# One attention stage of a four-block network: probabilities transposed on TensorE, or logits formed a second time with the keys on the partitions

## The chip, the cores and the metric

The kernel runs on one NeuronCore of a Trainium2 chip. The metric is the device time of one launch in microseconds, taken as the median of several runs. TensorE (PE) does the matrix products, VectorE (DVE), ScalarE (ACT) and GpSimd (POOL) the element-wise work, and SyncE (SP) issues the transfers.
## The reference, cut to what matters

The network is a chain of four blocks over `x` (4 batches, 512 tokens, 512 features). The changed stage is the attention of the third block. Its queries come from the 512 tokens of `x`, its keys and values from those tokens and 64 context tokens together, 576 keys in all, with 16 heads of 32 features:

```python
residual = latents                                  # x: 4 x 512 x 512
h = jnp.concatenate([x, latents], axis=1)           # context and tokens: 576 rows
q = (latents @ q_w + q_b).reshape(b, k_len, NH, DH)            # NH = 16, DH = 32
kv = (h @ kv_w + kv_b).reshape(b, p + k_len, NH, DH, 2)
attn = jnp.einsum('bkhd,bnhd->bhkn', q, kmat) / DH
attn = jnp.where(full_mask[:, None, None, :], attn, -jnp.inf)  # hides some context keys
attn = jax.nn.softmax(attn.astype(jnp.float32), axis=-1)
attn_out = jnp.einsum('bhkn,bnhd->bkhd', attn, v).reshape(b, k_len, H)
attn_out = attn_out @ out_w + out_b + residual
```

## The kernel before

The network is a list of stages, each ended by a barrier of all engines. The function `l2_attention_stage` is one of them; its tiles show in the trace without the 2 of their names (`l_slot`, `l_probs`). Its work is one loop of four passes, one a batch. In a batch the tokens are transposed into `source` (features on the partitions), and then four groups of four heads follow, `m` = 0 to 3. For each group `project` forms the queries and keys of 128 features, ACT copies them out of PSUM, and DVE (`split`) makes a rounded float32r part and the rest of each. SP copies these parts into `q_stack` and `k_stack`, 24 transfers a group (28 with the mask row, in the first group of a batch), so that for each head 96 partitions hold high, low and high parts one under another and one float32r product of 97 rows gives a logit of nearly float32 accuracy.

For each head `i` and each tile `t` of 128 queries, `logits` (L1021) makes a tile of 128 queries by 576 keys in two halves of 288 in one of two places of `slot`. DVE takes the maximum of each row (L1162), and ACT the exponential with that maximum as its bias (L1110), which also adds up the row. The values need the probabilities with the keys on the partitions, so TensorE turns them: `turn` (L1033) makes four transposes of 128 by 128 for each of five chunks of keys, and ACT (chunks 0, 2 and 4, L1133) and DVE (chunks 1 and 3, L1205) copy them out. `mix` (L1045) then multiplies a chunk with `padded_v`, a 128-wide copy of the values in which only the 32 columns of the head are not zero, so that four heads add up in one PSUM bank `gathered`. The sums of the rows are inverted while they are small (128 by 16, L1179), spread and turned once a group (`turn_inverse`, L1054), and multiplied in (L1190). At the end of a batch `project_out` (L1063) multiplies with `wo`; DVE adds the residual rows (L1218), and SP stores them.

The order on TensorE is written out by hand. Inside a head it alternates the logits of the next head, the transposes of this one and the values of the one before. The list of TensorE is that of the loops at the end of its block:

```python
for c in range(CHUNKS):
    if c < TPB and i + 1 < H:
        logits(b, i + 1, c)
    if i < H:
        turn(b, i, c)
    if i >= 1:
        mix(b, i - 1, c)
```

## Time and profile before

| what | us |
|---|---|
| median of 3 runs (3251.75 to 3257.56) | 3254.83 |
| the profiled execution, its own time | 3249.24 |
| its span in the profile | 3247.4 |
| TensorE busy in the span | 2958.6 (91%) |
| VectorE busy | 1538.0 (47%) |
| ScalarE busy | 938.5 (29%) |

The profile is of one execution. A busy time counts every instruction from its start to its modelled end, and matrix instructions overlap, so the distance between the starts of two instructions that follow each other without a wait tells what the first one costs the engine; the printed duration is longer. A printed group merges neighbours of one kind and gives their number after an x. The changed stage lies between 1370 and 2176 us of the span, a quarter of it.

### The profile page before, as it was taken

The numbers are of one execution on the slowest core, as the hardware profiler recorded it, in microseconds if no ns is written. First come the engines' busy times: TensorE is split into PE (matmuls) and PEld (weight loads), VectorE is DVE, ScalarE is ACT, GpSimd is POOL, SyncE is SP. The second block draws the span as 40 slices with busy tenths as digits, with TensorE's granted clock in tenths as the row PEclk, the third lists the DMA queues.
The fourth block names the chain that finished last, engine by engine and source line by source line (L and its number), as shares of the span: only waits on it lengthen the run. The fifth ranks groups of instructions, "written<-read, shape, count | busy, mean of one in ns | idle before, by whom it ended". The sixth has DMA issues, their size and how long they took to land. (4 is left out here: it accounts for less than half of the span.)

```text
span 3247.4 us, 34409 instructions
## 1 busy us (share of the span) xinstructions
PE 2958.6 (91%) x12408; PEld 2142.5 (66%) x12408; DVE 1538.0 (47%) x2345; ACT 938.5 (29%) x1914; POOL 177.0 (5%) x122
## 2 busy tenths in 40 slices
PE   6999979999979999899999999977999879779999
PEld 4776747777668887456465564646888635458887
DVE  3555454444674442236254463546444454564443
ACT  4223323333131111145254452533111112231111
POOL 2000001000040000000000000004000030021000
PEclk9999979999889999899999999998999999889999
DMA  3111011110010002122111221221000101110001
GB/s 128 40 52 52 0 56 52 53 52 1 1 56 26 26 1 88 38 55 57 48 43 49 59 52 55 47 74 55 26 27 1 56 24 39 59 68 27 26 1 52
DMA packets 63704, 139.72 MB, mean 43 GB/s; under 512 B 33298, under 2 KB 33427, under 8 KB 51795
## 3 DMA queue, kind: packets, MB, share of 16 engines
q1 hardware_dynamic: 46930, 137.52, 12.7%
q10 hardware_dynamic: 16640, 0.39, 0.2%
q8 instruction: 87, 1.43, 0.2%
q14 instruction: 47, 0.38, 0.0%
HBM read 82.89 MB, written 8.45 MB: 28 GB/s over the span
## 5 line engine op out<-in xcount | busy, mean ns | idle before, releaser
L1045 PE MATMUL l_gathered<-l_probs_T,l_padded_v 128*128 128x512 f32 x640 | 325.0, 594 | 0.0
L1162 DVE TENSOR_REDUCE l_top<-l_slot 128x1 f32<-128x576 f32 x256 | 192.5, 757 | 278.3 <-PE l_slot L1021 277.8
L1110 ACT ACTIVATE l_probs<-l_slot,l_top 128x576 f32<-128x576 f32 x256 | 190.0, 742 | 166.7 <-DVE l_top L1162 165.9
L1021 PE MATMUL l_slot<-l_k_stack,l_q_stack 128*128 128x288 f32 x512 | 192.7, 457 | 18.7 <-ACT l_probs L1110 16.2
L1033 PE MATMUL l_turned<-ident,l_probs 128*128 128x128 f32 x1280 | 193.4, 273 | 4.3 <-ACT l_probs_T L1133 4.3
L1033 PEld LDWEIGHTS l_turned<-ident,l_probs 128*128 128x128 f32 x1280 | 154.7, 140 | 50.2 <-ACT l_probs_T L1133 25.7
L1021 PEld LDWEIGHTS l_slot<-l_k_stack,l_q_stack 128*128 128x128 f32 x512 | 92.7, 190 | 128.7 <-issue 84.1
L470 PE MATMUL l0a_wide<-l0a_key_map,l0a_norm 128*128 128x260 f32 x512 | 118.7, 385 | 9.3 <-DVE l0a_soft L623 7.2
L470 PE MATMUL l0b_wide<-l0b_key_map,l0b_norm 128*128 128x260 f32 x512 | 118.7, 385 | 9.3 <-DVE l0b_soft L623 7.2
L1678 ACT ACTIVATE l2m_hidden<-l2m_up,columns 128x512 f32<-128x512 f32 x64 | 44.2, 692 | 270.1 <-PE l2m_up L131 263.9
L1678 ACT ACTIVATE l0m_hidden<-l0m_up,columns 128x512 f32<-128x512 f32 x64 | 44.0, 694 | 268.4 <-PE l0m_up L131 261.3
L1678 ACT ACTIVATE l3m_hidden<-l3m_up,columns 128x512 f32<-128x512 f32 x64 | 44.0, 694 | 268.4 <-PE l3m_up L131 261.3
L1133 ACT COPY l_probs_T<-l_turned 128x512 f32<-128x512 f32 x192 | 111.2, 579 | 25.3 <-PE l_turned L1033 19.1
L470 PEld LDWEIGHTS l0b_wide<-l0b_key_map,l0b_norm 128*128 128x128 f32 x512 | 95.6, 190 | 27.6 <-DVE l0b_soft L623 9.8
L470 PEld LDWEIGHTS l0a_wide<-l0a_key_map,l0a_norm 128*128 128x128 f32 x512 | 95.6, 190 | 27.6 <-DVE l0a_soft L623 9.8
L129 PE MATMUL l2m_up<-l2m_norm_hi,l2m_w1h 128*128 128x512 f32 x256 | 101.4, 396 | 8.4 <-DVE l2m_norm_lo L1742 8.4
L129 PE MATMUL l3m_up<-l3m_norm_hi,l3m_w1h 128*128 128x512 f32 x256 | 100.7, 394 | 7.1 <-DVE l3m_norm_lo L1742 7.1
L129 PE MATMUL l0m_up<-l0m_norm_hi,l0m_w1h 128*128 128x512 f32 x256 | 100.7, 393 | 7.1 <-DVE l0m_norm_lo L1742 7.1
L1045 PEld LDWEIGHTS l_gathered<-l_probs_T,l_padded_v 128*128 128x128 f32 x640 | 97.9, 191 | 10.5 <-issue 10.5
L130 PE MATMUL l2m_up<-l2m_norm_lo,l2m_w1h 128*128 128x512 f32 x256 | 100.8, 394 | 0.0
L131 PE MATMUL l2m_up<-l2m_norm_hi,l2m_w1l 128*128 128x512 f32 x256 | 100.6, 393 | 0.0
L130 PE MATMUL l0m_up<-l0m_norm_lo,l0m_w1h 128*128 128x512 f32 x256 | 100.3, 392 | 0.0
(369 smaller groups left out, 6314.4 us busy)
## 6 DMA issues: line engine op xcount, KB each, us to landing
l_k_stack<-l_k_parts SPq DMA_DIRECT2D x192, 72.0 KB, 2.0
l_q_stack<-l_q_parts SPq DMA_DIRECT2D x192, 64.0 KB, 2.0
l0m_raw<-in_weights SPq DMA_DIRECT2D x8, 1024.0 KB, 4.9
l_rows<-x SPq DMA_DIRECT2D x8, 1024.0 KB, 4.7
l2m_raw<-in_weights SPq DMA_DIRECT2D x8, 1024.0 KB, 7.0
l3m_raw<-in_weights SPq DMA_DIRECT2D x8, 1024.0 KB, 4.8
x<-in_x SPq DMA_DIRECT2D x4, 1024.0 KB, 9.4
l0a_wk<-in_weights SPq DMA_DIRECT2D x4, 1024.0 KB, 5.1
```

The lines of the kernel that those rows point to most:

```text
L129: pe.matmul(out, lh, rh, start=start, stop=False)
L130: pe.matmul(out, lh, rl, start=False, stop=False)
L131: return pe.matmul(out, ll, rh, start=False, stop=stop)
L470: last = pe.matmul(wide[:, j, 0:W], norm[:, k, at:at + P], key_map[:, k, b, :, :].rearrange("p h c -> p (h c)"), start=k == 0, stop=k == K ...
L1021: last = pe.matmul(out[:, half, 0:HALF], q_stack[:, j, t * P:(t + 1) * P], k_stack[:, j, half * HALF:(half + 1) * HALF], start=True, stop= ...
L1033: last = pe.transpose(turned[:, bank, t * P:(t + 1) * P], probs[:, i % 2, t, first:first + P], n.ident[:, :])
L1045: last = pe.matmul(gathered[:, m % 2, :], padded_v[:, c, j, :], probs_T[:, i % 2, c, :], start=(j == 0 and c == 0), stop=(j == 3 and c == ...
L1110: act.activation(probs[:, i % 2, t, :].rearrange("p (a k) -> p a k", a=2), slot[:, u % 2, :, 0:HALF], ACT.Exp, bias=top[:, i % 2, t:t + 1] ...
L1133: act.copy(probs_T[:, i % 2, c, :], turned[:, 0, :]).then_inc(s["turned0_out"], 1)
L1162: dve.tensor_reduce(top[:, i % 2, t:t + 1], slot[:, u % 2, :, 0:HALF], AX.XY, ALU.max, negate=True).then_inc(s["top_ready"], 1)
L1678: act.activation(hidden[:, i % 2, :], up[:, m, :], activation, bias=n.col(bias, f * KT + m))\
```

## The change

The loop over batches is written out, with groups numbered 0 to 15 through all batches (`g`). The logits are still formed with the queries on the partitions, in tiles of 128 by 576 (`logits`), but only to take the maxima; their place in `slot` is free once DVE has read it. The negated maxima of the four heads of a group are split into two float32r parts, turned by TensorE (`turn_tops`) and copied by ACT into rows 97 and 98 of `q_stack` (`take_tops`), where rows of ones in `k_stack` stand against them. A second product, `logits_across`, has the keys of a chunk as its stationary side and 512 queries moving, and so gives logit minus maximum with the keys on the partitions. ACT takes the exponential of a chunk of one head (128 keys by 512 queries) and writes it to `weighed`. The transposes of the probabilities, both kinds of copy out of `turned`, and `padded_v` are gone.

`mix` multiplies a chunk with the values of one head, 32 columns wide, into the 32 partitions of `gathered` that belong to the head, and then with 32 columns of ones into `totals`: eight products of 32 columns a chunk and group, where there were four of 128 columns. The reciprocal is taken of `totals`, 128 by 512, on DVE (`normalise`). The stacks have two halves, `g % 2`; SP fills the half of group `g + 2` once the last `logits_across` of group `g` is done, and TensorE waits for all transfers of a half at once. The mask row is loaded in the first two groups of a batch. The input is turned straight from `n.x`, GpSimd adds the bias to the residual rows, and DVE adds the value bias.

The diff, cut to its core:

```diff
...
-        stack_loaded = [n.sem(f"{tag}_stack{j}_loaded") for j in range(4)]
+        weighed = n.sbuf(f"{tag}_weighed", [P, RING, 4, S], F32, mem)
+        top = n.sbuf(f"{tag}_top", [P, TPB, 4], F32, mem)
+        top_parts = n.sbuf(f"{tag}_top_parts", [P, TPB, 4, 32], F32, mem)
+        inverse = n.sbuf(f"{tag}_inverse", [P, S], F32, mem)
+        slot = n.psum(f"{tag}_slot", [P, 4, 512], mem)
+        across = n.psum(f"{tag}_across", [P, 2, S], mem)
+        gathered = n.psum(f"{tag}_gathered", [P, S], mem)
...
+            def load_stack(g):
+                a, b, m = g % 2, g // GROUPS, g % GROUPS
+                sp.wait_ge(s["parts_ready"], g + 1)
+                if g >= 2:
+                    sp.wait_ge(s["across_done"], USES * (g - 1))
+                for j in range(4):
+                    mine = slice(32 * j, 32 * j + 32)
+                    for c in range(3):
+                        third = slice(32 * c, 32 * c + 32)
+                        sp.dma_start(q_stack[third, a, j, :].bitcast(F32), q_parts[mine, c // 2, :].bitcast(F32)).then_inc(stack_loaded[a], 16)
+                        sp.dma_start(k_stack[third, a, j, :].bitcast(F32), k_parts[mine, c % 2, :].bitcast(F32)).then_inc(stack_loaded[a], 16)
+                    if m < 2:
+                        sp.dma_start(k_stack[ROW:ROW + 1, a, j, S:KEYS].bitcast(F32),
+                                     mask[:, b * C:(b + 1) * C].bitcast(F32)).then_inc(stack_loaded[a], 16)
 
             sp.dma_start(keep[:, :], n.dram["keep_l2"]).then_inc(s["consts_loaded"], 16)
...
+            def turn_tops(g):
+                use = USES * g
+                pe.wait_ge(s["top_split"], g + 1)
+                if use:
+                    pe.wait_ge(s["across_read"], use - 1)
+                for t in range(TPB):
+                    last = pe.transpose(across[:, use % 2, t * P:(t + 1) * P],
+                                        top_parts[:, t, :, :].rearrange("p h c -> p (h c)"), n.ident[:, :])
+                last.then_inc(s["across_done"], 1)
+
+            def logits_across(g, c, j):
+                use = USES * g + 1 + 4 * c + j
+                pe.wait_ge(s["across_read"], use if c == 0 and j == 0 else use - 1)
+                pe.matmul(across[0:height(c), use % 2, :], k_stack[0:LAST, g % 2, j, keys_of(c)], q_stack[0:LAST, g % 2, j, :],
+                          start=True, stop=True).then_inc(s["across_done"], 1)
+
+            def mix(g, c):
+                m, tall = g % GROUPS, height(c)
                 if c == 0:
-                    pe.wait_ge(s["slot_read"], b * SLOTS + slot_of_logits(i, TPB - 1) + 3)
-                at = b * T1 + 2 * i + max(0, (i - 1) // 4) + c // 2 if bank else b * T0 + 3 * i + c // 2
-                pe.wait_ge(s[f"turned{bank}_out"], at + 1)
-                first = min(c * P, KEYS - P)
-                for t in range(TPB):
-                    last = pe.transpose(turned[:, bank, t * P:(t + 1) * P], probs[:, i % 2, t, first:first + P],
-                                        n.ident[:, :])
-                last.then_inc(s[f"turned{bank}_done"], 1)
-
-            def mix(b, i, c):
-                m, j = i // 4, i % 4
-                if c == 0:
-                    pe.wait_ge(s["padded_ready"], b * H + i + 1)
-                    pe.wait_ge(s["turned0_out"], b * T0 + 3 * i + 4)
-                    pe.wait_ge(s["turned1_out"], b * T1 + 2 * i + max(0, (i - 1) // 4) + 3)
-                    if j == 0:
-                        pe.wait_ge(s["gathered_read"], b * GATHERED + m + 1)
-                last = pe.matmul(gathered[:, m % 2, :], padded_v[:, c, j, :], probs_T[:, i % 2, c, :],
-                                 start=(j == 0 and c == 0), stop=(j == 3 and c == CHUNKS - 1))
-                if c == CHUNKS - 1:
-                    last.then_inc(s["gathered_done"], 1)
-
...
+            for g in range(ALL):
+                m, b = g % GROUPS, g // GROUPS
+                for c in range(CHUNKS):
+                    for j in range(4):
+                        logits_across(g, c, j)
+                        if c < TPB and g + 1 < ALL:
+                            logits(g + 1, TPB * c + j)
+                    if c:
+                        mix(g, c - 1)
+                if m == 1 and b + 1 < B:
+                    turn_input(b + 1)
+                if g + 3 < ALL:
+                    pe.wait_ge(s["top_ready"], TILES_OF * (g + 2))
+                    project_q(g + 3)
+                mix(g, CHUNKS - 1)
+                if g + 3 < ALL:
+                    project_k(g + 3)
+                if g + 1 < ALL:
+                    turn_tops(g + 1)
+                if m == GROUPS - 1:
...
+            def take_tops(g):
+                use = USES * g
+                act.wait_ge(s["across_done"], use + 1)
+                for j in range(4):
+                    last = act.copy(q_stack[ROW:LAST, g % 2, j, :], across[32 * j:32 * j + LAST - ROW, use % 2, :])
+                last.then_inc(s["across_read"], 1)
+
+            def exps(g, c):
+                if CHUNKS * g + c >= RING:
+                    act.wait_ge(s["mix_done"], CHUNKS * g + c - RING + 1)
+                for j in range(4):
+                    use = USES * g + 1 + 4 * c + j
+                    act.wait_ge(s["across_done"], use + 1)
+                    act.activation(weighed[0:height(c), (CHUNKS * g + c) % RING, j, :], across[0:height(c), use % 2, :], ACT.Exp)\
+                        .then_inc(s["across_read"], 1)
+
...
+            def split(g):
+                dve.wait_ge(s["k_out"], g + 1)
+                if g:
+                    dve.wait_ge(stack_loaded[(g - 1) % 2], loaded(g - 1))
                 dve.tensor_copy(q_parts[:, 0, :], projected[:, 0, 0:S])
-                dve.tensor_copy(k_parts[:, 0, :], projected[:, 1, :]).then_inc(s["parts_chain"], 1)
-                dve.wait_ge(s["parts_chain"], b * GROUPS + m + 1)
+                dve.tensor_copy(k_parts[:, 0, :], projected[:, 1, :]).then_inc(s["parts_high"], 1)
+                dve.wait_ge(s["parts_high"], g + 1)
                 dve.tensor_tensor(q_parts[:, 1, :], projected[:, 0, 0:S], q_parts[:, 0, :].bitcast(F32), ALU.subtract)
-                dve.tensor_tensor(k_parts[:, 1, :], projected[:, 1, :], k_parts[:, 0, :].bitcast(F32),
...
+            def split_tops(g):
+                dve.wait_ge(s["top_ready"], TILES_OF * (g + 1))
+                if g:
+                    dve.wait_ge(s["across_done"], USES * (g - 1) + 1)
+                dve.tensor_copy(top_parts[:, :, :, 1].bitcast(F32R), top[:, :, :]).then_inc(s["top_high"], 1)
+                dve.wait_ge(s["top_high"], g + 1)
+                dve.tensor_tensor(top_parts[:, :, :, 2], top[:, :, :], top_parts[:, :, :, 1], ALU.subtract).then_inc(s["top_split"], 1)
+
+            def normalise(g):
+                m, b = g % GROUPS, g // GROUPS
+                dve.wait_ge(s["mix_done"], CHUNKS * (g + 1))
+                dve.reciprocal(inverse[:, :], totals[:, :]).then_inc(s["inverse_ready"], 1)
+                dve.wait_ge(s["inverse_ready"], g + 1)
+                if b and m == 0:
+                    dve.wait_ge(s["out_done"], TPB * b)
+                dve.tensor_tensor(mixed[:, m, :], gathered[:, :], inverse[:, :], ALU.mult).then_inc(s["mixed_ready"], 1)
...
+            for g in range(ALL):
+                m, b = g % GROUPS, g // GROUPS
+                if g + 1 < ALL:
+                    for i in range(TILES_OF):
+                        maximum(g + 1, i)
+                    split_tops(g + 1)
+                normalise(g)
+                if g + 3 < ALL:
+                    split(g + 3)
+                if m == GROUPS - 1:
...
```

The order of instructions on TensorE. First the kernel before, inside one head: logits of the next head, transposes of this one, the values of the one before, and again.

```order
L1021 MATMUL l_slot<-l_k_stack,l_q_stack 128x288 x2
L1030 REGISTER_ALU
L1033 MATMUL l_turned<-ident,l_probs 128x128 x4
L1045 MATMUL l_gathered<-l_probs_T,l_padded_v 128x512
L976 REGISTER_ALU
L1021 MATMUL l_slot<-l_k_stack,l_q_stack 128x288 x2
```

The changed kernel, the end of one chunk and the beginning of the next one; a chunk has four such pairs of `l_across` and `l_slot`.

```order
L1032 MATMUL l_across<-l_q_stack,l_k_stack 128x512
L1015 MATMUL l_slot<-l_k_stack,l_q_stack 128x288 x2
L1032 MATMUL l_across<-l_q_stack,l_k_stack 128x512
L1015 MATMUL l_slot<-l_k_stack,l_q_stack 128x288 x2
L1044 MATMUL l_gathered<-l_weighed,l_values 32x512 x4
L1047 MATMUL l_totals<-l_weighed,l_ones 32x512 x4
L1032 MATMUL l_across<-l_q_stack,l_k_stack 128x512
```

The four transposes and the 128-wide product of each chunk and head have gone; a 512-wide product of the second logits has come in, and the values of four heads stand together as eight 32-wide products. At the end of a group TensorE now has these rows, from the last chunk (64 keys) on:

```order
L1032 MATMUL l_across<-l_q_stack,l_k_stack 64x512 x4
L1044 MATMUL l_gathered<-l_weighed,l_values 32x512 x4
L1047 MATMUL l_totals<-l_weighed,l_ones 32x512 x4
L967 MATMUL l_slot<-l_source,l_wq 128x512 x4
L1044 MATMUL l_gathered<-l_weighed,l_values 32x512 x4
L1047 MATMUL l_totals<-l_weighed,l_ones 32x512 x4
L975 MATMUL l_slot<-l_source,l_wk 128x288 x8
L1025 MATMUL l_across<-ident,l_top_parts 128x128 x4
L1032 MATMUL l_across<-l_q_stack,l_k_stack 128x512
L1015 MATMUL l_slot<-l_k_stack,l_q_stack 128x288 x2
```

The projections of a later group stand between the last values of a group and the turned maxima of the next; the row after the maxima, the first `l_across` of the next group, reads what ACT copies from them. On DVE the kernel before has this list where a group ends (`l_total` and `l_inverse` are 128 by 16, and the parts of a later group are split between the maxima):

```order
L1179 RECIPROCAL l_inverse<-l_total 128x16
L1180 ISA
L1181 COPY l_wide_inverse<-l_inverse 128x512
L1168 ISA
L1172 TENSOR_TENSOR l_padded_v<-l_values,l_bv_row 128x4x32
L1174 TENSOR_TENSOR l_padded_v<-l_values,l_bv_row 64x32
L1160 REGISTER_ALU
L1162 TENSOR_REDUCE l_top<-l_slot 128x1
```

And the changed kernel, one whole group:

```order
L1167 TENSOR_REDUCE l_top<-l_slot 128x1 x16
L1174 CAST l_top_parts<-l_top 128x16
L1176 TENSOR_TENSOR l_top_parts<-l_top,l_top_parts 128x16
L1181 RECIPROCAL l_inverse<-l_totals 128x512
L1185 TENSOR_TENSOR l_mixed<-l_gathered,l_inverse 128x512
L1151 CAST l_q_parts<-l_projected 128x512
L1152 CAST l_k_parts<-l_projected 128x576
L1154 TENSOR_TENSOR l_q_parts<-l_projected,l_q_parts 128x512
L1155 TENSOR_TENSOR l_k_parts<-l_projected,l_k_parts 128x576
```

The reciprocal has grown from 16 to 512 elements a partition, and it stands with the split of a later group ahead of the maxima of the next group but one.

## Rows read from the trace of the kernel before

**Rows 1.** Windows: busy us of each engine, TensorE's granted clock; the stage.

```profile
core 0: us, PE busy (x) PEld busy (x) DVE busy (x) ACT busy (x) POOL busy (x), PEclk, DMA share, GB/s
1370.00:2180.00 810.00, 761.78 (x3232) 468.05 (x3232) 384.19 (x661) 352.08 (x765) 7.65 (x4) 0.99 0.19 51
```

**Rows 2.** Timeline (start, us, instructions): the stage's first instruction and its last on DVE.

```profile
1369.86 1.80 POOL L963 MEMSET l_q_stack<- 32x2048 f32 x1 [399.88 <-POOLq L110]
...
2175.02 0.69 DVE L1218 TENSOR_TENSOR l_rows<-l_gathered,l_rows 128x512 f32<-128x512 f32 x1 [2.74 <-PE l_gathered L1063]
```

**Rows 3.** Costliest groups: busy us, mean ns of one, idle before and its releaser.

```profile
L1045 PE MATMUL l_gathered<-l_probs_T,l_padded_v 128*128 128x512 f32 x640 | 325.0, 594 | 0.0
L1162 DVE TENSOR_REDUCE l_top<-l_slot 128x1 f32<-128x576 f32 x256 | 192.5, 757 | 278.3 <-PE l_slot L1021 277.8
L1110 ACT ACTIVATE l_probs<-l_slot,l_top 128x576 f32<-128x576 f32 x256 | 190.0, 742 | 166.7 <-DVE l_top L1162 165.9
...
L1033 PE MATMUL l_turned<-ident,l_probs 128*128 128x128 f32 x1280 | 193.4, 273 | 4.3 <-ACT l_probs_T L1133 4.3
```

**Rows 4.** Timeline of TensorE in the stage's first batch, steady part and projections.

```profile
1442.60 0.82 PE L1021 MATMUL l_slot<-l_k_stack,l_q_stack 128*128 128x288 f32 x2
...
1444.15 0.83 PE L1021 MATMUL l_slot<-l_k_stack,l_q_stack 128*128 128x288 f32 x2
1444.82 0.60 PE L1033 MATMUL l_turned<-ident,l_probs 128*128 128x128 f32 x4
...
1446.12 0.60 PE L1033 MATMUL l_turned<-ident,l_probs 128*128 128x128 f32 x4
1446.55 1.02 PE L1045 MATMUL l_gathered<-l_probs_T,l_padded_v 128*128 128x512 f32 x2
1447.41 3.60 PE L1004 MATMUL l_slot<-l_source,l_wq 128*128 128x512 f32 x8
1450.85 4.04 PE L1009 MATMUL l_slot<-l_source,l_wk 128*128 128x288 f32 x16
1454.51 0.65 PE L1021 MATMUL l_slot<-l_k_stack,l_q_stack 128*128 128x288 f32 x2
```

**Rows 5.** Timeline of TensorE in the next stage: float32r products, 512 columns moving.

```profile
2211.54 0.39 PE L131 MATMUL l2m_up<-l2m_norm_hi,l2m_w1l 128*128 128x512 f32 x1
2211.77 0.39 PE L129 MATMUL l2m_up<-l2m_norm_hi,l2m_w1h 128*128 128x512 f32 x1
```

**Rows 6.** Timeline of TensorE in the first block: stationary data of 4 columns, then 128.

```profile
63.44 3.60 PE L452 MATMUL l0a_wide<-l0a_wo,l0a_learnt_v 128*4 128x512 f32 x8
66.97 2.00 PE L460 MATMUL l0a_wide<-l0a_keys,l0a_wqT 128*128 128x257 f32 x8
```

**Rows 7.** Groups by line: reciprocals on DVE, a copy on ACT.

```profile
L1179 DVE RECIPROCAL l_inverse<-l_total 128x16 f32<-128x16 f32 x16 | 4.0, 253 | 0.5
L822 DVE RECIPROCAL l_inverse<-l_total 128x4 f32<-128x4 f32 x4 | 0.7, 178 | 0.1
L1133 ACT COPY l_probs_T<-l_turned 128x512 f32<-128x512 f32 x192 | 111.2, 579 | 25.3 <-PE l_turned L1033 19.1
```

**Rows 8.** Timeline of DVE: start of a split, the instruction behind it, two maxima.

```profile
2098.24 0.43 DVE L1152 CAST l_q_parts<-l_projected 128x512 fp32r<-128x512 f32 x1
...
2100.35 0.68 DVE L1187 COPY l_inverse_T<-l_turned 128x512 f32<-128x512 f32 x1
...
2102.28 1.42 DVE L1162 TENSOR_REDUCE l_top<-l_slot 128x1 f32<-128x576 f32 x2
```

**Rows 9.** SP's queue: first and last of a group's 24 transfers; KB, us to landing.

```profile
1425.55 0.52 SPq L940 DMA_DIRECT2D l_q_stack<-l_q_parts  x1
...
1441.03 0.59 SPq L942 DMA_DIRECT2D l_k_stack<-l_k_parts  x1
l_k_stack<-l_k_parts SPq DMA_DIRECT2D x192, 72.0 KB, 2.0
```

**Rows 10.** Windows, columns as in rows 1: behind the first four logits tiles.

```profile
1409.00:1414.50 5.50, 5.34 (x10) 2.54 (x11) 0.56 (x3) 1.01 (x5) 0.00 (x0) 0.72 0.56 203
```

More of the change, by code:

```diff
@@ L904, in l2_attention_stage, with loaded, keys_of, height @@
+        def loaded(g):
+            return 16 * sum(24 + (4 if h % GROUPS < 2 else 0) for h in range(g % 2, g + 1, 2))
+        def keys_of(c):
+            return slice(c * P, min((c + 1) * P, KEYS))
+        def height(c):
+            return P if c < CHUNKS - 1 else C
         block = mem.enter_context(nc.Block())
@@ L1007, in project, with project_q, project_k @@
+            def project_q(g):
+                pe.wait_ge(s["source_ready"], 2 * (g // GROUPS + 1))
+                m = g % GROUPS
+                for k in range(KT):
+                    last = pe.matmul(slot[:, 0, :], wq[:, k, m * P:(m + 1) * P], source[:, k, 0:S], start=k == 0, stop=k == KT - 1)
+                last.then_inc(s["q_done"], 1)
+            def project_k(g):
+                pe.wait_ge(s["ctx_ready"], g // GROUPS + 1)
+                m = g % GROUPS
                 for half in range(2):
@@ new lines, in add_out @@
+            def add_out(b):
+                dve.wait_ge(s["rows_ready"], TPB * (b + 1))
+                for t in range(TPB):
+                    dve.wait_ge(s["out_done"], TPB * b + t + 1)
+                    dve.tensor_tensor(rows[:, t, :], slot[:, OUT_BANK[t], :], rows[:, t, :], ALU.add).then_inc(s["out_added"], 1)
+            split(0)
+            take_values(0)
+            split(1)
+            for i in range(TILES_OF):
+                maximum(0, i)
+            split_tops(0)
+            split(2)
```

416 lines of the change are left out of this document (157 added, 259 removed).

## The prediction

> **What bounds the kernel now.** I read the windows of the changed stage first, then its edges, the costliest groups, and the timeline of TensorE in its steady part. In the stage TensorE is busy 762 of 810 us at a granted clock of 0.99, VectorE 384 and ScalarE 352 [rows 1]: the stage is TensorE's. It runs from 1369.9 to 2175.7 us, 806 us [rows 2]. DVE's maxima wait 278 us for TensorE, and ACT's exponentials 166 us for DVE, while the costliest products wait for nothing [rows 3].
>
> In the steady part each step is read from the distance of two starts [rows 4]. Four transposes and one 128-wide float32 product of 512 columns (two instructions) follow each other at 1446.12, 1446.55 and 1447.41: 0.43 to 0.44 and 0.86 us. With a pair of logits products the round is 1.55 where without it is 1.30 (1444.82 to 1446.12): 0.26 for the pair. A query projection is 3.44, a key projection 3.66. So TensorE's own time in the stage is: 320 products of values at 0.86 = 275; 320 times four transposes at 0.44 = 141; 256 logits tiles at 0.26 = 67; 16 query and 16 key projections 55 + 59; value and output projections, 20 and 16 times eight instructions of 0.43, 69 + 55; input and inverse transposes 14. That is 735, and 806 - 735 leaves 71 us of waits and edges.
>
> **What goes and what comes on TensorE.** Transposes and 128-wide products of values go: -416 us. The other 319 us stay; the turned maxima replace the turned inverses one for one.
>
> The second logits are 320 float32r products with 512 columns moving. In the next stage two such products start 0.23 us apart [rows 5]: +74. Bounds: half of a float32 instruction's 0.43, so 0.21, and 0.30 if the change between products costs something; 67 to 96.
>
> The values are now 640 float32 products of 32 columns, 1280 instructions. This is the term that decides, and no row shows products that write different 32-column strips. The sum of TensorE is 319 + 74 + 291 = 684, 51 below before. Although the transposes are gone, the values cost 291 instead of 275, because the sums of the rows are now products too.
>
> The Trainium skill, "TensorE: Matmul & The Clock Gate", Part 3, says that column strips run concurrently with starts some 4 ns apart and gives 2.38x for three 32-wide products, but also that matrix instructions start and end strictly in program order. By the first sentence alone the stage would come out as in the four-at-once rival; by the second it comes out as forecast. No row here shows either.
>
> **What TensorE now waits for.** Durations come from rows; hand-overs (0.3 us from issue to a result, 0.1 for a semaphore) are estimates, since no row has this pattern. ACT's exponential of 512 columns lies between the copy of 512 (579 ns) [rows 7] and the exponential of 576 (742) [rows 3]: 0.69, repeated every 0.60. Maxima repeat every 0.66 (1.42 for two, 0.76 for one) [rows 3, 8].
>
> (a) The turned maxima. The first product across of a group reads what ACT copies from them: the key projection's copy (about 0.65) must be done, then four copies of 512 columns at 0.49 each. TensorE has 0.43 us of other work. It idles 2.75 us in 13 groups; in the other three the value and output projections cover it: 36.
> (b) Inside a chunk TensorE issues a pair of steps in 0.49, but both `across` and `slot` have two places. After two free steps the third waits 0.4 for the first exponential, the fourth 0.3 for the second maximum: 0.69 in 48 chunks = 33. The chunk of 64 keys has no logits beside it and goes at ACT's pace, 1.3 in 16 groups = 21; the last group has none at all, 4. Together 58. During the values (3.64) ACT and DVE catch up, so neither becomes the bound: DVE's list is 16 x 0.66 + 0.5 + 3.35 + 0.7 + 2.1 = 17 a group of some 42.
> (c) The start of a group on DVE and SP. A reciprocal of 16 elements takes 253 ns and of 4 178 [rows 7]: 6.25 ns an element, so 3.35 us for 512 (bounds 0.7, the price of a multiplication of that size, and 4). It, the multiplication and the split (2.11) [rows 8] stand ahead of the maxima of the next logits. The reciprocal is hidden by the key projection (3.66), the turned maxima and wait (a). The split is not: it waits for the same transfers as the logits. SP issues 24 in 1441.03 - 1425.55 + 0.6 = 16.1 us, landing 2.0 after issue [rows 9], so 17.5 to 18 us (28 of them: some 20) behind the last product across. TensorE comes to the logits after 3.64 + 3.44 + 3.64 + 3.66 + 0.43 + 2.75 + 0.23 = 17.8. So the logits start about in time or 2 us late, and the maxima 2 us behind that: 3 us in each of 12 groups, 35. Bounds 0 and 80: at 0.8 us a transfer instead of 0.64 each group would start 4 us later.
> (d) Ends. Input copies 4 x 1.6; the first 16 logits tiles stand alone at DVE's pace and cost 9 more than their issue; last reciprocal, multiplication and addition 6, others 2: 23.
>
> Waits are 36 + 58 + 35 + 23 = 152. The stage is 684 + 152 = 836 against 806: +30. ACT loses copies and row sums, which frees nothing, since TensorE does not wait for their absence. GpSimd's additions (16) and context copies lie beside TensorE's list. The profiled execution of 3249 becomes 3279; it lies 5.6 us below the median, so I add the difference to the median: 3254.8 + 30 = 3285.
>
> **Rivals.**
> *Four strips at once (faster).* Each half product of a head runs beside those of the other three, as though each strip had its own list. Place: the eight products at the end of a chunk. They cost 1.72 + 0.2, so TensorE's sum is 684 - 80 x 1.72 = 546. But the road to the logits of the next group is now 3.4 us shorter than the transfers, so (c) grows by some 30 to 65, and the waits to 182. The stage is 728, -78: 3177. It decides from a chunk below 3.3 us: with 80 chunks the 30 us are made up at 0.37 us a chunk. For it speaks that the stage gives each head its own 32 partitions of both banks; against it that the two halves of a float32 product stand next to each other in TensorE's list. The page named above, read for concurrency alone, says this rival.
> *Nothing overlaps.* The eight products cost 6.88 + 0.2, +275; (c) falls by 20, since the transfers are now covered: 836 + 255 = 1091 or, with more of (b) left open, up to 1100: 3254.8 + 290 = 3545. For it: the rows know only full serial products [rows 4, 6]. Against it: 32-row strips of one bank have no shared output.
> *The clock.* As forecast, but TensorE, idle more often, gets the lower clock. Behind the four sparse logits tiles at the start of the first batch the granted clock of the next 5.5 us was 0.72 [rows 10], where full speed would have saved some 1.5 of them. If each group pays 1.5 to 2 us so: +25 to 30, 3312. The whole stage had 0.99 though [rows 1], and the gaps of (a) and (c) are 3 us.
> *Less waiting than counted.* (a), (b) and (c) rest on hand-overs. If they were half, the stage would equal the one before: 3255 +- 6.
>
> The Trainium skill, "TensorEngine Tiling (Array Packing)", Key Properties, says that a change of tiling mode drains TensorE. Here the trace agrees in kind and has 0.1 us for it [rows 6], which is in the sum; with the 0.3 of the bound the sum would be 16 us more.
>
> **Chances and range.** Two at once, with its clock variant: 0.48 (own range 3265 to 3312). Four at once: 0.28. Nothing overlaps: 0.20. Less waiting: 0.04. What this kernel's measurement can tell from no change is 0.2%, 6.5 us. Faster takes the 0.28, half of the last case and 0.02 of the first: 0.32; the same 0.05; slower 0.63. The range reaches from four at once to the clock variant, 3165 to 3315, and leaves out the serial case.
>
> **What would show it.** In the changed trace: the distance of starts inside the eight 32-wide products (0.43 a product says forecast, 0.86 serial, about 0.2 four at once); the distance between two chunks, 6.3 us; groups 41 to 45 us long; the first `l_across` of a group waiting 2.7 us for ACT's copies into `l_q_stack`; `l_inverse` near 3.4 us; the stage 836 us long; the stages around it unchanged. The forecast falls if a chunk's values take under 3.3 or over 4.2 us, if the granted clock of the stage is below 0.95, or if the transfers land more than 20 us behind the last product across.

## The result and the profile after

| what | before | after |
|---|---|---|
| median of 4 runs, us | 3253.8 | 3215.0 (3212.9 to 3220.7) |
| ratio to before (95% interval) | | 0.9887 (0.9868 to 0.9905) |
| span of the profiled execution | 3247.4 | 3211.1 |
| the changed stage, from its first instruction to its last | 806 | 765 |
| TensorE busy in the windows of the stage | 762 | 662 |

The changed kernel is 39 us faster, and the stage is 41 us shorter in the profile; the forecast was 30 us slower. The stage's first instruction and its last on DVE, which answer to the two in [rows 2]:

```profile
1371.27 0.31 SPq L915 DMA_DIRECT2D l_keep<-in_keep_l  x1
...
2135.55 0.69 DVE L1191 TENSOR_TENSOR l_rows<-l_slot,l_rows 128x512 f32<-128x512 f32 x1 [2.74 <-PE l_slot L998]
```

The windows of the kernel after, with the columns of [rows 1]: the whole stage, the stretch ahead of the first product across, then twice the first stretch of a group (its first eight steps and first values) with the stretch that follows.

```profile
1370.00:2136.00 766.00, 662.21 (x2912) 334.70 (x2912) 316.27 (x422) 250.28 (x425) 33.54 (x26) 0.89 0.16 40
1370.00:1445.24 75.24, 60.57 (x164) 33.57 (x164) 26.35 (x37) 8.72 (x13) 17.35 (x11) 0.80 0.21 52
1445.24:1454.89 9.65, 9.65 (x40) 6.06 (x41) 5.93 (x8) 4.69 (x8) 0.00 (x0) 0.65 0.01 2
1454.89:1480.80 25.91, 22.61 (x125) 10.74 (x121) 10.03 (x12) 10.45 (x18) 0.40 (x1) 1.00 0.23 57
1557.91:1572.21 14.30, 9.81 (x40) 6.88 (x40) 8.03 (x12) 4.78 (x8) 0.00 (x0) 0.64 0.12 29
1572.21:1597.00 24.79, 24.24 (x129) 11.63 (x126) 10.02 (x12) 9.37 (x17) 0.00 (x0) 1.00 0.21 51
```

The granted clock of the stage fell from 0.99 [rows 1] to 0.89. The loss sits ahead of the first product across (0.80) and at the starts of groups: 0.65 and 0.64 there, 1.00 directly behind. The page's groups answer to [rows 3, 7]: a maximum costs what it did (754 ns, before 757), an exponential of 512 columns 595 ns (forecast 690), and the 512-element reciprocal came at 3357 ns (forecast 3350). TensorE now waits for ACT's copies of the turned maxima and for transfers.

```profile
L1123 ACT ACTIVATE l_weighed<-l_across 128x512 f32<-128x512 f32 (+1 forms) x320 | 182.7, 595 | 282.1 <-PE l_across L1032 275.3
L1167 DVE TENSOR_REDUCE l_top<-l_slot 128x1 f32<-128x576 f32 x256 | 184.0, 754 | 84.7 <-PE l_slot L1015 77.6
L1032 PE MATMUL l_across<-l_q_stack,l_k_stack 99*128 99x512 f32 (+1 forms) x320 | 156.2, 500 | 45.8 <-ACT l_q_stack L1114 35.2
...
L1181 DVE RECIPROCAL l_inverse<-l_totals 128x512 f32<-128x512 f32 x16 | 53.7, 3357 | 175.7 <-PE l_totals L1047 175.7
```

The page names only the first releaser of the logits. The view by line, for the stage alone, names three; the two DMA entries make 29.4 us.

```profile
L1015 PE MATMUL l_slot<-l_k_stack,l_q_stack 97*128 97x288 f32 x512 | 147.7, 378 | 41.1 <-DMA l_k_stack<-l_k_parts 16.8 <-DMA l_k_stack<-l_mask 12.6 <-DVE l_top L1167 7.5
```

The timeline of TensorE at the start of the first batch's fourth group answers to [rows 4].

```profile
1557.91 0.50 PE L1032 MATMUL l_across<-l_q_stack,l_k_stack 99*128 99x512 f32 x1 [2.76 <-ACT l_q_stack L1114]
1562.12 0.85 PE L1015 MATMUL l_slot<-l_k_stack,l_q_stack 97*128 97x288 f32 x2 [3.71 <-DMA l_k_stack<-l_mask]
...
1572.21 0.50 PE L1032 MATMUL l_across<-l_q_stack,l_k_stack 99*128 99x512 f32 x1
1572.55 0.43 PE L1015 MATMUL l_slot<-l_k_stack,l_q_stack 97*128 97x288 f32 x2
...
1574.96 1.06 PE L1044 MATMUL l_gathered<-l_weighed,l_values 128*32 128x512 f32 x8
1575.84 1.04 PE L1047 MATMUL l_totals<-l_weighed,l_ones 128*32 128x512 f32 x8
1576.81 0.50 PE L1032 MATMUL l_across<-l_q_stack,l_k_stack 99*128 99x512 f32 x1
```

A chunk goes from 1572.21 to 1576.81, 4.60 us: 2.75 of steps and 1.85 of values (0.88 and 0.97). The forecast had 2.65 (four times 0.26 + 0.23, and 0.69 of hand-overs) and 3.64. Cut into a shorter window (1570.30 to 1570.80), the same trace merges only what starts in it:

```profile
1570.36 0.64 PE L1044 MATMUL l_gathered<-l_weighed,l_values 128*32 128x512 f32 x4
```

Four instructions lie within 0.64 us. Two on one strip start 0.43 apart (one_strip, below), so these are one of each head, and all four strips stream at once.

### The profile page after: what moved, and what is told of

Same layout as the page of the kernel before. It is cut to its first block and busy times, and to the rows that moved or that the text cites. A ratio compares the mean times of both kernels' runs of the same rounds, so it can differ in the third digit from the quotient of the medians.

```text
span 3211.1 us, 31363 instructions
## 1 busy us (share of the span) xinstructions
PE 2862.9 (89%) x12088; PEld 2011.8 (63%) x12088; DVE 1465.2 (46%) x2105; ACT 837.3 (26%) x1574; POOL 207.1 (6%) x144
## 5 line engine op out<-in xcount | busy, mean ns | idle before, releaser
L1123 ACT ACTIVATE l_weighed<-l_across 128x512 f32<-128x512 f32 (+1 forms) x320 | 182.7, 595 | 282.1 <-PE l_across L1032 275.3
L1167 DVE TENSOR_REDUCE l_top<-l_slot 128x1 f32<-128x576 f32 x256 | 184.0, 754 | 84.7 <-PE l_slot L1015 77.6
L1032 PE MATMUL l_across<-l_q_stack,l_k_stack 99*128 99x512 f32 (+1 forms) x320 | 156.2, 500 | 45.8 <-ACT l_q_stack L1114 35.2
L1015 PE MATMUL l_slot<-l_k_stack,l_q_stack 97*128 97x288 f32 x512 | 147.7, 378 | 41.1 <-DMA l_k_stack<-l_k_parts 16.8
L1015 PEld LDWEIGHTS l_slot<-l_k_stack,l_q_stack 97*128 97x128 f32 x512 | 110.1, 236 | 82.0 <-DVE l_top L1167 36.6
L1032 PEld LDWEIGHTS l_across<-l_q_stack,l_k_stack 99*128 99x128 f32 (+1 forms) x320 | 66.7, 213 | 115.1 <-issue 42.8
L1181 DVE RECIPROCAL l_inverse<-l_totals 128x512 f32<-128x512 f32 x16 | 53.7, 3357 | 175.7 <-PE l_totals L1047 175.7
L131 PE MATMUL l0m_up<-l0m_norm_hi,l0m_w1l 128*128 128x512 f32 x256 | 100.4, 392 | 0.0
L130 PE MATMUL l3m_up<-l3m_norm_lo,l3m_w1h 128*128 128x512 f32 x256 | 100.3, 392 | 0.0
```

What stands on the lines that cost most here:

```text
L130: pe.matmul(out, lh, rl, start=False, stop=False)
L131: return pe.matmul(out, ll, rh, start=False, stop=stop)
L1015: last = pe.matmul(slot[:, 2 * (i % 2) + half, 0:HALF], q_stack[0:ROW + 1, g % 2, j, t * P:(t + 1) * P], k_stack[0:ROW + 1, g % 2, j, half ...
L1032: pe.matmul(across[0:height(c), use % 2, :], k_stack[0:LAST, g % 2, j, keys_of(c)], q_stack[0:LAST, g % 2, j, :], start=True, stop=True).t ...
L1123: act.activation(weighed[0:height(c), (CHUNKS * g + c) % RING, j, :], across[0:height(c), use % 2, :], ACT.Exp)\
L1167: dve.tensor_reduce(top[:, i % TPB, i // TPB:i // TPB + 1], slot[:, 2 * (i % 2):2 * (i % 2) + 2, 0:HALF], AX.XY, ALU.max, negate=True).the ...
```

## The experiments

Each kernel ran on a chip beside the kernel before, whose medians there were 3252.4 to 3255.7 us. Where no interval is given there was one run.

### Are strips what counts? All values into one strip, or two

```diff
-pe.matmul(gathered[32 * j:32 * j + 32, :], values...
+pe.matmul(gathered[0:32, :], values...                                    # one_strip
+pe.matmul(gathered[32 * (j % 2):32 * (j % 2) + 32, :], values...         # two_strips
```

The same holds for `totals`. What several heads write to one strip is added up there, so the output is no longer that of the attention; shapes, counts and order stay. The reciprocal and the multiplication read only the rows that are written.

> The changed kernel with all eight 32-wide products of a chunk written to the same strip, partitions 0 to 31 of `gathered` and of `totals`, instead of one strip a head (the values of the four heads are then added up in one strip, so the output is not the attention's; shapes, counts and order stay). Theory S (the four strips run side by side, whatever the two halves of a float32 product): the eight products go from 1.85 us to 16 x 0.43 = 6.9 us a chunk, 80 chunks, +400 us, of which some 20 to 60 come back because the transfers and the slow clock at the start of a group are covered: 3555 to 3600 us. Theory N (a product with 32 stationary columns is cheap by itself, wherever it writes): 1.85 us stays, 3215 us.

> As one_strip, with heads 0 and 2 in the first strip and heads 1 and 3 in the second. Theory S: two run at a time, 3.45 us a chunk, +128 us, 20 to 60 of them given back: 3280 to 3325 us. If only the second half of one product and the first half of the next could overlap (the step of the forecast), two strips would do all that four can and the time would stay at 3215. Theory N: 3215.

Measured: 3572.4 and 3313.8 us. TensorE in one_strip:

```profile
1607.87 3.62 PE L1045 MATMUL l_gathered<-l_weighed,l_values 128*32 128x512 f32 x8
1611.33 3.60 PE L1048 MATMUL l_totals<-l_weighed,l_ones 128*32 128x512 f32 x8
1614.86 3.70 PE L968 MATMUL l_slot<-l_source,l_wq 128*128 128x512 f32 x8
```

And in two_strips:

```profile
1601.05 1.91 PE L1045 MATMUL l_gathered<-l_weighed,l_values 128*32 128x512 f32 x8
1602.79 1.89 PE L1048 MATMUL l_totals<-l_weighed,l_ones 128*32 128x512 f32 x8
1604.61 0.67 PE L1033 MATMUL l_across<-l_q_stack,l_k_stack 99*64 99x512 f32 x2
```

The eight products take 6.99 us in one strip, 3.56 in two and 1.85 in four: time goes as the number of products a strip gets. One strip is 357 us slower than four; 80 x (6.99 - 1.85) is 411. Of the 54 between, 35 are waits that the longer chunks cover: the 29.4 for transfers are gone, and those for the maxima fell from 7.5 to 1.9. The other 19 were not separated; the granted clock between the first and the last reciprocal is 0.97 there and 0.90 in the changed kernel. Both runs came out in the ranges of theory S. My forecast of 3.64 is what two strips give.

### Does the order of the products in the list count?

```diff
-                for j in range(4):        # second loop, totals
                     last = pe.matmul(totals[32 * j:32 * j + 32, :], ones...   # now directly behind head j's gathered product
```

> The changed kernel with the eight products of a chunk in another order: values and ones of head 0, then of head 1, and so on, so that two products for the same strip follow each other; same work. Theory Q (each strip takes its products as it comes free, past products that wait for another strip): 1.85 us a chunk stays, 3215 us. Theory L (products start in the order of the list; the four ran side by side only because neighbours in the list were for different strips): the products of a head must start before those of the next one, 13 times 0.43 = 5.6 us a chunk, +300 us less 20 to 50 of cover: 3465 to 3495 us; or, if halves of two neighbours are exchanged, about 3.4 us a chunk and 3320 us.

Measured: 3207.6 us, and no slower chunk. That is 7 us below the changed kernel, from one run; why is open.

```profile
1576.10 1.08 PE L1044 MATMUL l_gathered<-l_weighed,l_values 128*32 128x512 f32 x8
1576.98 1.06 PE L1046 MATMUL l_totals<-l_weighed,l_ones 128*32 128x512 f32 x8
1577.97 0.50 PE L1032 MATMUL l_across<-l_q_stack,l_k_stack 99*128 99x512 f32 x1
```

In the list, all four instructions of head 0 now stand ahead of those of head 1. Yet the eight instructions of `gathered` lie within 1.08 us, and the first of `totals` starts 0.88 behind the first of them: the value products of head 3 start before the sum of head 0, which stands 11 places ahead of the last of them in the list. The chunk takes 1.87. So a product that waits for its strip doesn't hold back those behind it for other strips. This is the step of the forecast that failed. The Trainium skill, "TensorE: Matmul & The Clock Gate", Part 3, has the concurrency (the trace agrees: 6.99 / 1.85 = 3.8 for four strips); its strict program order of starts doesn't hold between strips here.

### Is a narrow product cheaper by itself? Narrow values in the kernel before

```diff
-last = pe.matmul(gathered[:, m % 2, :], padded_v[:, c, j, :], ...
+last = pe.matmul(gathered[32 * j:32 * j + 32, m % 2, :], padded_v[:, c, j, 32 * j:32 * j + 32], ...
```

> The kernel before with 32-wide products of values only (the 32 columns of padded_v that are not zero, into the 32 partitions of the head) and everything else as it was: one product at a time between transposes, so no neighbour in another strip. Theory S (the gain lies in strips side by side): none here; 320 products change the width twice, 0.1 us each time, +64 us at most and 0 at least if the change costs nothing here: 3255 to 3320 us. Theory N (narrow products are cheap): 0.86 to 0.2 us each, -200 us.

Measured: 3329.8 us, ratio 1.0232 (1.0215 to 1.0249), 75 us slower than before and 10 us above the upper end of theory S.

```profile
1440.34 1.04 PE L1045 MATMUL l_gathered<-l_probs_T,l_padded_v 128*32 128x512 f32 x2
1441.31 0.53 PE L1021 MATMUL l_slot<-l_k_stack,l_q_stack 128*128 128x288 f32 x2
1441.68 0.60 PE L1033 MATMUL l_turned<-ident,l_probs 128*128 128x128 f32 x4
1442.21 1.05 PE L1045 MATMUL l_gathered<-l_probs_T,l_padded_v 128*32 128x512 f32 x2
1443.18 0.66 PE L1033 MATMUL l_turned<-ident,l_probs 128*128 128x128 f32 x4
1443.77 1.04 PE L1045 MATMUL l_gathered<-l_probs_T,l_padded_v 128*32 128x512 f32 x2
```

The product takes 0.97 instead of 0.86, the logits pair 0.37 instead of 0.26, the transposes 0.53 instead of 0.43, and 0.59 where they stand between two narrow products. A round takes 1.87 and 1.56 for 1.55 and 1.30 [rows 4]: the two changes of width cost 0.32 and 0.26, more than the 0.2 that [rows 6] gave, and enough for the 10 us above the range. A 32-column product saves nothing alone. In the changed kernel it pays with three others beside it, and the two changes are paid once for eight products.

### What the sums of the rows cost

The products with the columns of ones are left out of four chunks in five; the output is then not that of the reference.

```diff
-for j in range(4):                      # totals
+for j in range(4 if c == 0 else 0):
```

> The changed kernel, but the sums of the rows are formed from the first chunk of keys alone: the products with the 32 columns of ones of chunks 1 to 4 are left out (the output is not that of the reference). It measures what the sums cost TensorE. Theory P (they cost what their starts show, 0.92 us for four strips side by side, and TensorE is the bound): 64 x 0.92 = 59 us less, but the transfers of the next group now land up to 0.9 us later against TensorE's list in 8 to 12 groups, some 9 more: 3215 - 50 = 3165 (3155 to 3172). Theory R (without them VectorE's maxima and ScalarE's exponentials set the pace of a chunk: 4 x 0.66 = 2.64 a chunk against 2.75 + 0.92): the chunk is still TensorE's, so nothing more is lost; if the hand-overs count, a chunk takes 4.1 instead of 3.67 and the whole 3190.

Measured: 3179.3 us, 36 less, of 59 of TensorE's time, and 7 us above the range of theory P. TensorE's group of logits in the stage:

```profile
L1015 PE MATMUL l_slot<-l_k_stack,l_q_stack 97*128 97x288 f32 x512 | 147.8, 380 | 57.1 <-DMA l_k_stack<-l_k_parts 26.2 <-DMA l_k_stack<-l_mask 16.3 <-DVE l_top L1167 10.8
```

Waits for transfers are 42.5 us (29.4 after), those for the maxima 10.8 (7.5): 16 of the 23 us that are missing. I expected 9. Most of the rest is slower work: between the first and the last reciprocal lie 60 of the 64 chunks, 55 us of sums, but TensorE's busy time falls only from 558.2 to 507.7 us, 50, at a granted clock of 0.88 instead of 0.90.

### Filling the wait for the turned maxima

```diff
 def logits_across(g, c, j):
+    if c == 0 and j == 0 and (g % GROUPS or g == 0):
...
+        for _ in range(12):
+            pe.matmul(across[:, use % 2, :], k_stack[0:ROW, g % 2, j, 0:P], q_stack[0:ROW, g % 2, j, :], start=True, stop=True)
```

> The changed kernel with 12 float32r products of 512 columns (results overwritten by the next product) put into TensorE's wait for ACT's copies of the maxima, in the 13 groups where it waits 2.76 us; the wait itself stays as long. Theory C (the idle time costs more than itself: it lets the clock fall, and the first chunk of the group runs at half speed): the first chunk of a group goes from 9.6 to 14 us down to 5 to 11, 2 to 3 us saved in each of 13 groups, 3175 to 3195 us, granted clock of the stage above 0.93 where it was 0.89. Theory W (only the waits cost, the clock would have fallen anyway): 3215 us within 4, clock 0.89.

Measured: 3208.4 us, ratio 0.9859 (0.9843 to 0.9876), 7 us below the changed kernel's 3215.0, though the intervals of the two ratios overlap. It fits neither theory: C had 3175 to 3195, W 3211 to 3219. In group 0, where no transfer is waited for, it works:

```profile
1444.69 2.99 PE L1035 MATMUL l_across<-l_q_stack,l_k_stack 96*128 96x512 f32 x12
1447.69 0.50 PE L1038 MATMUL l_across<-l_q_stack,l_k_stack 99*128 99x512 f32 x1
...
1455.06 0.50 PE L1038 MATMUL l_across<-l_q_stack,l_k_stack 99*128 99x512 f32 x1
```

The first stretch takes 7.37 us where it took 9.65 after. In groups that then wait for transfers (2.31 us at 1483.80) the clock falls all the same. That second wait hides what the first costs, so the last experiment below repeats the test without it.

### Which wait ends last? Turned maxima ahead of the key projection

```diff
-project_k(g + 3)
 turn_tops(g + 1)
+project_k(g + 3)          # ACT copies in the same order
```

> The changed kernel with the turned maxima of the next group ahead of the key projection (3.7 us) instead of behind it, and ACT's copies of them ahead of the key projection's copy: the wait of 2.76 us in 13 groups has cover. If TensorE's waits add up: -36 us, of which the transfers of the stacks, which are then waited for 2.8 us longer in 8 groups, take back 22: 3200 us. With theory C the granted clock also rises where no transfer is waited for (5 groups, 2 to 3 us each): 3185 us. Theory W: 3200 us.

Measured: 3208.2 us, ratio 0.9854 (0.9837 to 0.9871), again with an interval that touches the changed kernel's; expected were 3200 or 3185. The wait for the turned maxima fell from 35.2 to 4.9 us, but that for transfers rose from 29.4 to 57.1 (expected was a rise of 22), and that for late maxima from 7.5 to 14.0:

```profile
L1032 PE MATMUL l_across<-l_q_stack,l_k_stack 99*128 99x512 f32 (+1 forms) x320 | 155.2, 497 | 15.6 <-ACT l_weighed L1126 10.2 <-ACT l_q_stack L1117 4.9
L1015 PE MATMUL l_slot<-l_k_stack,l_q_stack 97*128 97x288 f32 x512 | 147.6, 378 | 75.6 <-DMA l_k_stack<-l_k_parts 34.8 <-DMA l_k_stack<-l_mask 22.3 <-DVE l_top L1175 14.0
```

SP's queue shows why. In the kernel after, the logits of the next group, which start at 1562.12, need 28 transfers, from here to here:

```profile
1543.38 0.51 SPq L909 DMA_DIRECT2D l_q_stack<-l_q_parts  x1
...
1560.40 0.59 SPq L912 DMA_DIRECT2D l_k_stack<-l_mask  x1
```

The first is issued 0.5 us behind the start of the last product across (1542.85), the last at 1560.40, and TensorE's logits follow at 1562.12. That moment hangs on this product, which SP waits for, and not on what TensorE does in between.

### Waiting for one head's transfers, and the split off the start of the group

```diff
-pe.wait_ge(stack_loaded[g % 2], loaded(g))          # all heads, at i == 0
+pe.wait_ge(stack_loaded[g % 2][j], loaded(g))       # head j, at its t == 0
 for i in range(TILES_OF):
     maximum(g + 1, i)
+    if i == 11 and g and g + 2 < ALL:
+        split(g + 2)                                # was behind the maxima: split(g + 3)
```

> The changed kernel with the transfers of the stacks counted by head: TensorE waits for the 6 or 7 transfers of a head before that head's logits instead of for all 24 or 28 before the first, and DVE splits the parts of a later group behind twelve of the sixteen maxima instead of ahead of them. Theory D (the wait for all transfers at once, and the slow clock behind it, is where the four-at-once sum was missed): TensorE's 29 us of waits for transfers in 8 groups go, and of the slow clock behind them 2 to 3 us a group, 20 us more: 3160 to 3175 us. Theory T (the wait for the turned maxima is enough for the clock to fall): only the 29 us and DVE's 8: 3180 us, granted clock of the stage still about 0.90.

Measured: 3167.7 us, ratio 0.9732 (0.9715 to 0.9748), 47 us below the changed kernel, and no wait of TensorE for a transfer is left. That is more than the 29.4 of those waits. The stretch between the first and the last reciprocal is 44 us shorter (642.1 to 598.6): TensorE idles 33 us less, among them the waits for late maxima (0.78 us in seven groups), and is busy 10 us less with the same instructions, at 0.94 of the clock instead of 0.90. No run has one of the two edits without the other.

### Both edits

The edits of tops_early and of by_head in one kernel.

> by_head and tops_early together: neither the transfers nor the copies of the maxima are waited for. Both theories: the 36 us of waits for the copies go besides the 29 us for the transfers, and with no long wait left in a group the clock stays up, granted clock of the stage above 0.97: 3215 - 29 - 36 - 30 to 40 = 3110 to 3120 us. If the parts only add up as measured alone (tops_early gave 7 us), 3160 us and more.

Measured: **3134.6 us, ratio 0.9635 (0.9619 to 0.9651)**, the fastest here, 120 us below the kernel before. Each edit alone gave 47 and 7 us, together 80: turning the maxima early pays once the transfers don't take over its wait. Windows with the columns of [rows 1], the stage and the first stretch of the second group:

```profile
1370.00:2057.50 687.50, 635.64 (x2913) 305.57 (x2912) 312.17 (x422) 248.30 (x425) 33.55 (x26) 0.95 0.18 45
...
1478.23:1486.64 8.41, 7.57 (x43) 3.91 (x41) 5.67 (x9) 5.32 (x9) 0.40 (x1) 1.00 0.27 68
```

It came out 15 to 25 us above what was expected, and the clock of the stage at 0.95 (above 0.97 was expected; between the first and the last reciprocal it is 0.98). The reciprocals show a regular group:

```profile
1508.74 3.36 DVE L1191 RECIPROCAL l_inverse<-l_totals 128x512 f32<-128x512 f32 x1 [13.24 <-PE l_totals L1048]
1540.12 3.36 DVE L1191 RECIPROCAL l_inverse<-l_totals 128x512 f32<-128x512 f32 x1 [10.06 <-PE l_totals L1048]
```

31.38 us, of which TensorE waits 1.2. Its first stretch takes 8.41 us at full clock (the window above); in the last experiment below, with the maxima turned in their old place, it takes 7.42. The difference comes with the edit itself. ACT now copies the key projection last, and the logits need the place in `slot` that it reads:

```profile
1478.64 0.74 ACT L1111 ACTIVATE l_projected<-l_slot,columns 128x576 f32<-128x576 f32 x1 [1.55 <-PE l_slot L975]
1479.48 0.50 PE L1016 MATMUL l_slot<-l_k_stack,l_q_stack 97*128 97x288 f32 x2 [0.65 <-issue]
```

The logits start 0.10 us behind the end of that copy. At 1.0 us in each of 13 groups this is 13 of the missing 15 to 25 us.

### The clock by itself: by_head with the wait filled

The edit is that of fill_gap, made in by_head. The wait stays; the fill lies inside it.

> This is by_head (waits per head, split of the next parts in the middle of the maxima) with twelve products of 97 rows, whose result nobody reads, put ahead of the first product across of 13 groups. They take 2.8 to 3.0 us at full clock and stand where TensorE otherwise waits 2.76 us for ACT's copies of the turned maxima, so they add no work to the path. The wait itself stays. Theory K (an idle TensorE is granted a lower clock afterwards, and that is a cost of its own): with by_head the distance of two reciprocals in the middle of a batch was 35.1 to 35.3 us against 31.4 in the version that has neither wait, 3.8 more, of which the wait is 2.76; the 1.1 left in each group and the 2.3 of group 0 are the clock. Filled, the distance becomes 34.2 and the whole 3167.7 - 12 x 1.1 - 2.3 = 3152 (3148 to 3158). Theory N (what is left is other hand-overs, the clock only goes with them): 3166 to 3172, distance 35.1 to 35.4.

Measured: 3150.1 us, ratio 0.9681 (0.9664 to 0.9697), 18 us below by_head, as theory K had it. Windows of by_head: the first stretch of its third group, which has a wait of 2.76 us ahead of it, and a part of that stretch.

```profile
1519.47:1528.63 9.16, 9.16 (x41) 6.52 (x41) 6.04 (x8) 4.67 (x8) 0.00 (x0) 0.63 0.00 0
1520.78:1526.46 5.68, 5.68 (x20) 4.95 (x19) 4.78 (x7) 3.74 (x7) 0.00 (x0) 0.50 0.00 0
```

The same stretch in head_fill, and from its timeline what stands in the place of the wait:

```profile
1516.03:1523.45 7.42, 7.37 (x40) 4.00 (x41) 5.62 (x8) 4.67 (x8) 0.00 (x0) 1.00 0.01 2
```

```profile
1513.03 2.96 PE L1036 MATMUL l_across<-l_q_stack,l_k_stack 96*128 96x512 f32 x12
1516.03 0.50 PE L1039 MATMUL l_across<-l_q_stack,l_k_stack 99*128 99x512 f32 x1
```

With the wait the stretch takes 9.16 us at a mean of 0.63, which is 6.8 us at 0.50, the lower of the clock's two levels (1.2 GHz of 2.4); with products in its place it takes 7.42 at 1.00. The distance of two reciprocals in mid-batch is 33.6 us against 35.1 to 35.9. Between the first and the last reciprocal the granted clock of head_fill is 1.00. Idling can make TensorE pay twice: the wait, then the slow clock behind it.

It does not always. Of the 13 filled waits by_head has one, of 2.76 us as well, behind which the clock stayed up:

```profile
1824.89:1832.31 7.42, 7.37 (x40) 3.99 (x40) 5.61 (x8) 4.67 (x8) 0.00 (x0) 1.00 0.11 26
```

That stretch takes the 7.42 us of head_fill with its wait still there. What decides it no run shows; over the 13 groups the slow clock makes the 18 us between the two runs, 1.4 a group.

## Why the prediction was wrong, point by point

- **Values, the step that failed.** "TensorE starts its list in order. So only the second half of one head's product can run beside the first half of the next head's." The order of the list binds only within a strip: 1.85 us a chunk, not 3.64, and 80 x 1.79 = 143 us less. The direction was decided here, as the text said ("This is the term that decides"); the rival "four strips at once" had the mechanism, at 0.28.
- **Removed transposes and wide products, second logits.** The terms held: no `l_turned` is left, and a chunk's steps take 2.75 us with hand-overs (forecast 2.65).
- **(a) Turned maxima.** 2.76 us in 11 groups and 2.43 in 2, 35.2 in all; forecast 2.75 in 13, 36.
- **(b) Hand-overs.** Too small, in two ways. The 0.69 a chunk was counted in 48 chunks, but 15 groups have four chunks with logits beside them, 60: 8 us more. And a regular group of head_fill, at full clock and without a wait for transfers, takes 33.55 us, where the forecast's terms with 1.85 for the values and 0.69 in all four chunks give 32.35 (logits 16 x 0.26, products across 20 x 0.23, projections 3.44 + 3.66, values 5 x 1.85, hand-overs 4 x 0.69 + 1.3, turned maxima and wait 0.43 + 2.75). Of the 1.20 between, 0.52 lie in the projections (3.63 and 3.99; they now stand beside narrow products), 0.51 in the chunks and 0.17 at the turned maxima. x16 this is 19 us.
- **(c) Transfers.** The size came out, the places did not. Forecast were 35 us in 12 groups; measured are 29.4 us of waits for transfers in 8 groups and 5.6 for the late maxima behind them. 24 transfers land 17.1 to 18.3 us behind the start of the last product across (forecast 17.5 to 18), 28 of them 19.3 to 20.1. TensorE comes to the logits after 15.4, and after 18.6 in the three groups with the input transposes of the next batch, which therefore don't wait. So mid-stage groups wait 1.6 to 2.4 us, with 28 transfers 3.7 to 4.5. The last logits alone wait 9.1, since no projection stands ahead of them. The growth of 30 to 65 us that the rival with shorter values had did not come.
- **The clock.** It was a variant, priced 25 to 30 us on 1.5 to 2 a group, and set aside because the stage before had 0.99 and the gaps would be 3 us. It came at that price. Between the first and the last reciprocal the changed kernel takes 642.1 us and `both` 561.4, with the same number of matrix instructions; of the 80.7 between, 52.8 are idle time of TensorE, and 28 are busy time, the same work at a lower clock. 2.3 in group 0 make 30. From 1445 to 2120 us the stage before had 1.00, and no wait of TensorE longer than 1.7 us; that says nothing of a stage with waits of 2.8. "The forecast falls if ... the granted clock of the stage is below 0.95": it was 0.89.
- **Ahead of the first product across** 75.2 us passed at 0.80. A clock at its lower level for 0.4 of them costs at most half of that, 15: an estimate, no run tried it.
- **The price of a wider bound.** With 0.3 for each of the two changes of width in a chunk the forecast's sum would be 32 us more, not 16.

The sum: 836 - 143 - 1 (a and c) + 8 + 19 (b) + 30 + 15 = 764, where 765 was measured. So close a fit is partly chance, since the 15 is a bound and the 19 takes one regular group for all. The forecast's 3285 and the result's 3215 thus differ by one wrong mechanism worth 143 us, and by three costs of 72 us, sized too small or left out of the sum, that hid half of it. That the result lay inside the range is owed to this and was luck. The rival with the right mechanism was not exact either: its 3177 is 38 us too low, for it lacked the same three costs and had the transfers too dear.

## What to carry to other kernels

Products of 32 columns that write four different strips stream together, in both orders of the list that were run, and nothing else that was tried made them pay: gather them between wide products. When a stage loses work on its bounding engine, look which wait ends last at each hand-over. Of two waits with one end, removing the first alone gave 7 us, hardly more than the spread of the runs, the second alone 47, and both together 80. A wait of 2.4 to 2.8 us on TensorE cost another 1.4 us on average in the clock behind it, in single groups 0 to 2.3, so a stage's clock before the change is no argument once the change adds waits.

## What was not expected of the hardware

- Eight float32 products with 32 stationary columns and 512 moving take 6.99 us in one strip, 3.56 in two, 1.85 in four, and 1.87 in four when each strip's instructions stand together in the list.
- Around a lone narrow product between wide ones the product itself and the steps beside it take 0.10 to 0.11 us more each, and transposes between two narrow products 0.16; in the kernel before this made 75 us for 320 products.
- After a wait of 2.76 us the granted clock was still full for the first 0.8 us of new work in by_head (to 1520.3) and then low to 1527.1; behind one of 13 such waits it stayed up. With products in the wait's place, which nobody reads, it stayed up in every group.
- A reciprocal of 128 x 512 on DVE takes 3357 ns, 6.26 ns for each element beyond 16, where 4 and 16 elements had said 6.25 [rows 7]; it is hidden here, since DVE waits some 11 us for the sums ahead of it.
